# W1 kept raw and split per batch in the expert half of a graph-attention and mixture-of-experts kernel; b2 in three parts; the last GELUs ahead of a norm

## What is computed

```
Wh = layernorm(x) @ W.T
e  = leaky_relu(Wh@a1 [:,None] + Wh@a2 [None,:], 0.2), masked by adj > 0
x1 = x + elu(softmax(e) @ Wh)
xn = layernorm(x1)
two experts per batch: top 2 of softmax(rescaled softmax(mean(xn) @ Wr + br))
h  = gelu(xn @ W1[expert] + b1[expert]);  y = h @ W2[expert] + b2[expert]
out = x1 + layernorm(sum of gate * y + xn) * gamma + beta
```

## Time and profile before

| | us |
|---|---|
| median of 3 runs | 295.44 (293.95 to 296.98) |
| the profiled execution's own time | 294.31 |
| its span, first to last instruction | 292.5 |
| TensorE busy in it | 253.4 |
| VectorE busy in it | 234.6 |
| ScalarE busy in it | 222.7 |
| GpSimd busy in it | 154.2 |
| mean granted TensorE clock | 0.975 |

### The profile page before, as it was taken

How to read it: one execution, slowest core, us unless ns; L and a number is a source line. 1 busy time by engine, 2 the same in 40 slices (tenths; PEclk the granted TensorE clock), 3 DMA queues, 4 the chain that set the end, 5 groups by cost and what they waited for, 6 DMA issues and landing times.

```text
span 292.5 us, 6644 instructions
## 1 busy us (share of the span) xinstructions
PE 253.4 (87%) x1844; PEld 227.5 (78%) x1845; DVE 234.6 (80%) x668; ACT 222.7 (76%) x509; POOL 154.2 (53%) x239
## 2 busy tenths in 40 slices
PE   5639998999788989999987599499999999999962
PEld 3639987888778878899976347489999999999952
DVE  4297999999999999999997564607778767788756
ACT  2257898998988899999997449277878878888370
POOL 5242187788988897787548712112234432223544
PEclk9977999999999999999999979989999999999999
DMA  6999366543366236440000014832454445545222
GB/s 101 216 197 200 72 111 108 106 89 73 63 108 106 52 63 109 72 75 1 2 1 2 0 39 133 301 106 84 171 180 162 161 146 177 180 163 171 64 72 74
DMA packets 40670, 31.51 MB, mean 108 GB/s; under 512 B 2400, under 2 KB 36608, under 8 KB 40640
## 3 DMA queue, kind: packets, MB, share of 16 engines
q1 hardware_dynamic: 31936, 21.72, 23.3%
q0 software_dynamic: 8704, 9.45, 20.6%
HBM read 27.48 MB, written 4.20 MB: 108 GB/s over the span
## 4 chain that ended last, share of the span: by engine, by line
PE 38%; ACT 5%; issue 4%; POOL 3%; DVE 3%; SPq 3%; DMA 2%; POOLq 0%; DVEq 0%; ACTq 0%
PE banks L1359 16%; PE banks L1344 4%; PE banks L1346 4%; PE banks L1345 4%; PE banks L1222 4%; DMA w_pair<-w_parts 2%; ACT leaky L966 2%; PE banks L1175 1%; PE banks L1207 1%; POOL rstd L429 1%; PE banks L1199 1%; ACT leaky L1113 1%; ACT h_att L976 1%; SPq L321 1%; SPq L330 1%
## 5 line engine op out<-in xcount | busy, mean ns | idle before, releaser
L1222 PE MATMUL banks<-whx,prob_t 128*128 128x129 f32 x512 | 68.2, 277 | 3.7 <-ACT h_att L976 2.5
L1222 PEld LDWEIGHTS banks<-whx,prob_t 128*128 128x128 f32 x512 | 62.0, 192 | 6.8 <-issue 5.7
L416 POOL TENSOR_SCALAR x_all<-x_all,rstd,nb 128x128 f32<-128x128 f32 x60 | 44.2, 748 | 3.1 <-POOL nb L405 3.1
L1207 PE MATMUL banks<-ident,logit 128*128 128x128 f32 x256 | 37.6, 281 | 4.9 <-DVE logit L570 4.1
L481 POOL TENSOR_SCALAR veps<-mv 128x4 f32<-128x4 f32 x15 | 5.9, 393 | 64.0 <-DVE mv L834 64.0
L1001 ACT ACTIVATE prob_t<-banks 128x512 f32<-128x512 f32 x64 | 38.3, 638 | 0.9 <-PE banks L1207 0.8
L1103 ACT ACTIVATE logit<-logit,nb,rstd 128x128 f32<-128x128 f32 x60 | 24.8, 484 | 17.3 <-POOL nb L486 17.3
L1207 PEld LDWEIGHTS banks<-ident,logit 128*128 128x128 f32 x256 | 30.3, 145 | 6.2 <-DVE logit L570 6.0
L399 POOL TENSOR_TENSOR rstd<-var,minus_half 128x8 f32<-128x8 f32 (+1 forms) x20 | 33.7, 1684 | 0.4
L1344 PE MATMUL banks<-x2t_hi,w_pair 128*128 128x512 f32 x64 | 27.3, 426 | 4.1 <-DMA w_pair<-w_parts 3.9
L1359 PEld LDWEIGHTS banks<-w2s,masked_even 128*128 128x128 f32 x256 | 29.7, 192 | 0.5
(11 more groups left out here) (149 smaller groups left out, 560.8 us busy)
## 6 DMA issues: line engine op xcount, KB each, us to landing
adj_sb<-in_adj_dram POOLq DMA_DIRECT2D x16, 512.0 KB, 6.9
w_pair<-w_parts SPq DMA_DIRECT2D x30, 256.0 KB, 2.3
x_all<-in_x_dram SPq DMA_DIRECT2D x16, 256.0 KB, 2.8
w2r<-in_L_ffn_W_dram SPq DMA_DIRECT2D x32, 128.0 KB, 2.1
out_dram<-prob_t SPq DMA_DIRECT2D x15, 256.0 KB, 2.3
w_parts<-in_L_ffn_W_dram SPq DMA_DIRECT2D x1, 1024.0 KB, 9.2
b_mix<-b_spread POOLq DMA_DIRECT2D x1, 768.0 KB, 7.5
b_mix<-b_spread POOLq DMA_DIRECT2D x1, 256.0 KB, 4.2
```

Of the source, the lines that this page charges most:

```text
L416: nc.gpsimd.tensor_scalar(x_all[:, b, tile], x1_all[:, b, tile], rstd12[c % 4][:, 1, t:t + 1], nb2[c % 2][:, t:t + 1], ALU.mult, ALU.add). ...
L1207: last = nc.tensor.transpose(lt_ps[t % 2][:, c * P:(c + 1) * P], logit[:, t, c * P:(c + 1) * P], ident[:])
L1222: last = nc.tensor.matmul(into[:, 0:D + 1], prob_t[:, t, c * P:(c + 1) * P], whx[b % 3][:, c, 2:WHX], start=(c == 0), stop=(c == T - 1))
```

## The change

1. `w1_parts` becomes `w1_all`, the raw W1. The four splits on ScalarE and the four on GpSimd in the attention half are gone.
2. SyncE's load_w1 fetches the two chosen experts' raw W1 from DRAM into `w1_raw[batch % 2]`, 128 KB each. Two waits ahead of its first load are gone, and the load of batch b now waits for the low split of batch b-2.
3. ScalarE makes the high parts of a pair (`split_w1_hi`, 128x2x256) in step n for batch n+2, behind the GELUs of batch n+1. VectorE makes the low parts (`split_w1_lo`) in step n for batch n+2, behind aggregate3(n) and ahead of add_b2(n+2).
4. hidden_part(b) waits for the low split of batch b instead of for a DMA. Batch 0 has its own function (`first_hidden_part`): both products with the high part of W1 first, the four products with the low part at the end. Its raw weights are copied by GpSimd, its high parts made by ScalarE, straight from w1_all.
5. b2 goes out in three parts: batches 0 and 1, 2 to 4, and 5 to 15, the third one behind norm3(0).
6. The four GELUs of batch 15 stand ahead of norm_z(13).

```diff
             def load_w1(b):
                 par = b % 2
                 if b >= 2:
-                    sp.wait_ge(s_hid_ps, KC * (b - 1))
+                    sp.wait_ge(s_w1lo, b - 1)
                 for k in range(TOP_K):
                     e = sp.value_load(top_idx[b:b + 1, k:k + 1], min_val=0, max_val=E - 1)
-                    sp.dma_start(w1_pair[par][:, k].bitcast(F32), w1_parts[:, e].bitcast(F32)).then_inc(s_w1[par], 16)
+                    sp.dma_start(w1_raw[par][:, k, :], w1[e]).then_inc(s_w1[par], 16)
...
-            sp.wait_ge(s_w1lo, 4)
-            sp.wait_ge(s_x2t_ps, B)
             sp.wait_ge(s_idx, 1)
...
             for n in range(B + 1):
                 step(n)
-                if 5 <= n < 9:
-                    split_w1_lo(n - 5)
...
+            for k in range(TOP_K):
+                e = pool.value_load(top_idx[0:1, k:k + 1], min_val=0, max_val=E - 1)
+                nc.gpsimd.tensor_copy(w1_raw[0][:, k, :], w1_all[:, e]).then_inc(s_pick, 1)
...
             def step2(half, n):
                 if in_range(half, n):
                     norm3(half, n)
+                if isinstance(half, int) and n == 0:
+                    load_b2(2)
...
+            def split_w1_lo(half, n):
+                b, h, par = batch_at(half, n)
+                if isinstance(half, int) and b == 0:
+                    dve.wait_ge(s_pick, TOP_K)
+                if past(half, b, 2):
+                    dve.wait_ge(s_hid_ps, KC * (b - 1))
+                dve.wait_ge(s_w1hi, b + TOP_K)
+                nc.vector.tensor_tensor(w1_pair[par][:, :, 1, :], w1_raw[par][:], w1_pair[par][:, :, 0, :].bitcast(F32),
+                                        ALU.subtract).then_inc(s_w1lo, 1)
...
             router_steps["gated"] = rc[0]
+            split_w1_lo(0, 0)
...
             split_x2t_lo(0, 2)
+            split_w1_lo(0, 1)
...
                     split_x2t_lo(half, n + 3)
                 if in_range(half, n):
                     aggregate3(half, n)
+                if in_range(half, n + 2):
+                    split_w1_lo(half, n + 2)
                 if in_range(half, n + 2):
                     add_b2(half, n + 2)
...
-                if 4 <= n < 8:
-                    split_w1_hi(n - 4)
...
+            for k in range(TOP_K):
+                e = act.value_load(top_idx[0:1, k:k + 1], min_val=0, max_val=E - 1)
+                nc.scalar.copy(w1_pair[0][:, k, 0, :], w1_all[:, e]).then_inc(s_w1hi, 1)
...
+            def split_w1_hi(half, n):
+
+                b, h, par = batch_at(half, n)
+                act.wait_ge(s_w1[par], 32 * h + 32 * par)
+                if not isinstance(half, int) or b >= 2:
+                    act.wait_ge(s_hid_ps, KC * (b - 1))
+                nc.scalar.copy(w1_pair[par][:, :, 0, :], w1_raw[par][:]).then_inc(s_w1hi, 1)
...
             def step2(half, n):
                 if in_range(half, n + 1):
                     apply_gelu(half, n + 1)
+                if in_range(half, n + 2):
+                    split_w1_hi(half, n + 2)
                 if in_range(half, n + 3):
                     split_hi(half, n + 3)
...
             scale_w2(0, B - 1)
+            apply_gelu(0, B - 1)
             norm_z(0, END - 1)
-            apply_gelu(0, B - 1)
             norm_z(0, END)
...
-            def hidden_part(half, n, between=(None,) * KC):
+            def hidden_part(half, n):
                 b, h, par = batch_at(half, n)
-                first = isinstance(half, int) and b == 0
-                if not first:
-                    pe.wait_ge(s_w1[par], 32 * h + 32 * par)
                 pe.wait_ge(s_x2lo, b + 1)
+                pe.wait_ge(s_w1lo, b + 1)
```

More of the change, by code:

```diff
@@ L129, in gat_moe_kernel @@
         b2_spread = nc.dram_tensor("b2_spread", [B, D], F32, kind="Internal")
-        w1_parts = sb("w1_parts", [P, E, 2, F], F32R)
+        w1_all = sb("w1_all", [P, E, F])
+        w1_raw = [sb(f"w1_raw{i}", [P, TOP_K, F]) for i in range(2)]
         w2r = [sb(f"w2r{i}", [P, TOP_K, FC, D]) for i in range(2)]
@@ L215, in gat_moe_kernel @@
         s_b2_out = sem("b2_rows_spread")
-        s_b2mix = [sem("b2_mix_loaded0"), sem("b2_mix_loaded1")]
+        s_b2mix = [sem(f"b2_mix_loaded{i}") for i in range(3)]
         s_n2e = sem("norm2_end_chain")
-        s_pick = [sem("first_w1_copied0"), sem("first_w1_copied1")]
+        s_pick = sem("first_w1_copied")
         s_x1b = sem("x1b_ready")
@@ L417, in scale_x2 @@
                                             nb2[c % 2][:, t:t + 1], ALU.mult, ALU.add).then_inc(s_x2, 1)
[L419 to L423, removed]
             def norm2_last_tile(t):
@@ L465, in _, with load_b2 @@
             pool.wait_ge(s_b2_out, 16)
-            for i, part in enumerate((slice(0, B2_FIRST), slice(B2_FIRST, B))):
+            def load_b2(i):
+                part = slice(B2_PARTS[i], B2_PARTS[i + 1])
                 nc.gpsimd.dma_start(b2_mix[:, part, :], b2_spread[part, :].rearrange("(a b) d -> a b d", a=1).to_broadcast(
                     [P, part.stop - part.start, D])).then_inc(s_b2mix[i], 16)
+            load_b2(0)
+            load_b2(1)
             def norm3(half, n):
@@ L796, in add_b2 @@
                 b, h, par = batch_at(half, n)
-                if isinstance(half, int) and b == B2_FIRST:
-                    dve.wait_ge(s_b2mix[1], 16)
+                if isinstance(half, int) and b in B2_PARTS[1:3]:
+                    dve.wait_ge(s_b2mix[B2_PARTS.index(b)], 16)
                 nc.vector.tensor_tensor(x_all[:, b, :].rearrange("p (t d) -> p t d", t=T),
@@ L1326, in mix_b2 @@
                 nc.tensor.matmul(r2_ps[0:B, 128:128 + D], w_dense_t[:], b2_sb[:], start=True, stop=True).then_inc(s_rps, 1)
-            def hidden_part(half, n, between=(None,) * KC):
+            def first_hidden_part(between):
+                pe.wait_ge(s_x2lo, 1)
+                for kc in range(KC):
+                    k, columns = kc // FC, slice(kc % FC * P, (kc % FC + 1) * P)
[3 more added lines that the diff above has]
+                    nc.tensor.matmul(hid_ps[kc], hi, x2t_lo[0][:], start=False, stop=False)
+                    if between[kc] is not None:
+                        between[kc]()
+                pe.wait_ge(s_w1lo, 1)
+                for kc in range(KC):
+                    k, columns = kc // FC, slice(kc % FC * P, (kc % FC + 1) * P)
+                    nc.tensor.matmul(hid_ps[kc], w1_pair[0][:, k, 1, columns], x2t_hi[0][:], start=False,
+                                     stop=True).then_inc(s_hid_ps, 1)
+            def hidden_part(half, n):
                 b, h, par = batch_at(half, n)
-                first = isinstance(half, int) and b == 0
-                if not first:
-                    pe.wait_ge(s_w1[par], 32 * h + 32 * par)
                 pe.wait_ge(s_x2lo, b + 1)
+                pe.wait_ge(s_w1lo, b + 1)
                 for kc in range(KC):
                     k, c = kc // FC, kc % FC
-                    if first and c == 0:
-                        pe.wait_ge(s_pick[k], 1)
-                    if not isinstance(half, int) or b >= 1:
-                        pe.wait_ge(s_hid, KC * (b - 1) + kc + 1)
+                    pe.wait_ge(s_hid, KC * (b - 1) + kc + 1)
                     columns = slice(c * P, (c + 1) * P)
@@ L1347, in hidden_part @@
                                      stop=True).then_inc(s_hid_ps, 1)
-                    if between[kc] is not None:
-                        between[kc]()
             def out_part(half, n):
```

19 lines of the change are left out of this document (6 added, 13 removed).

## The result

The changed kernel takes 368.19 us (median of 4 runs, 367.87 to 369.5), the kernel before 295.73 us (median of 4, one more than in the table above, 293.95 to 296.98): ratio 1.246, 95% interval 1.239 to 1.254. Forecast were 359 us with a range of 342 to 374; the time is inside the range and 9 us over the forecast, nearest to rival 1 (367 us). The profiled execution took 369.5 us and has a span of 367.7.

What follows compares the result with a forecast made beforehand. The prediction took the expert half to be bound by TensorE alone. From 294.3 us: -3.9 (attention half), +4.7 (entry), +50.4 (waits), +13.8 (clock), 0 (end) gave 359.3, say 359 us; range 342 to 374.

Steps and rivals of the forecast that it cites:

- rival 1: Expert half: the clock falls in every gap, 1.8 us each, 367 us in all; chance 0.20.
- the closed chain: Expert half, each batch: output(n), sum_z(n), four more VectorE groups, W1 low part, hidden(n+2); 4.2 us.
- 4.2 us per batch, 12 new waits, none for hidden(15): Expert half: TensorE waits for W1's low part, 12 x 4.2 = 50.4 us new; hidden(15)'s wait near 0.
- The clock, 1.2 us a gap: Expert half: slow clock after 13 gaps, 15.6 us less 1.8 paid today, +13.8 us (bounds -1.8 to +21.6).
- The upper value of 1.8: Expert half: most slow-clock time per gap, in us, from nine matmuls 0.43 us apart instead of 0.23 to 0.24.
- ScalarE's copy and the raw loads at nothing: Expert half: ScalarE's high part per batch and SyncE's W1 loads from DRAM are ready early; cost 0.
- The attention half, -3.9 us: Attention half: without ScalarE's four copies and GpSimd's four subtracts, -3.9 us (bounds -2.0 to -3.9).
- rival 4: Attention half gives nothing, as another engine holds its beat at the same length: 363 us; chance 0.04.
- the lower bound of -2.0: Attention half: the gain in us if only ScalarE's copies count.
- The entry, +4.7 us: Start of expert half: hidden(1) waits 2.8 us for W1's low part, GELUs 2 us late; bounds +2.5 to +6.5.
- The end, 0: Kernel's end: last GELUs could start some 3 us earlier, but VectorE's tail needs norm_z(14); 0 (bounds -3 to +0.6).
- Rival 3, faster: Expert half: W1's low part ready before output(n) ends, beat stays 6.33 us, 289 us; chance 0.03.

Runs made afterwards that it cites:

- experiment 1: Changed kernel with VectorE's low split of W1 for batch n+2 moved ahead of sum_z(n): 291.73 us, ratio 0.989 to the kernel before.
- experiment 3: Changed kernel with the low split of W1 directly behind sum_z(n), ahead of add_beta: 324.68 us, ratio 1.101 to the kernel before.
- experiment 2: Changed kernel with 14 idle matmuls on TensorE ahead of each hidden product from batch 1 on, results unused: 345.3 us, ratio 1.171.
- experiment 4: On experiment 1, four 128x512 copies on ScalarE put back into the attention half, output unread: 292.29 us.
- experiment 5: On experiment 1, four 128x512 subtracts on GpSimd put back into the attention half, output unread: 294.74 us, ratio 0.996.
- experiment 6: On experiment 1, both ScalarE's four copies and GpSimd's four subtracts put back into the attention half, outputs unread: 295.43 us, ratio 0.997.
- experiment 8: On experiment 1, W1's splits for batch 1 and the low split for batch 2 moved earlier in the entry: 286.92 us, ratio 0.970.
- experiment 7: On experiment 1, the last four GELUs put back behind norm_z(13), as in the kernel before: 293.0 us, ratio 0.991.
- experiment 9: On experiment 8, b2's rows sent out in two parts (batches 0 to 3 and 4 to 15), both at once: 285.87 us, ratio 0.965.
- experiment 10: On experiment 8, eight idle matmuls in TensorE's pauses inside hidden(0), results unused: 287.59 us, ratio 0.972.

## Why the prediction was right, and where its size was off

**What bounds the half; the closed chain.** Right. TensorE bound it before (busy 87.35 of 87.40 us); experiment 1 shows that the order alone breaks it, and experiment 3 that the loss follows the length of the chain: four groups fewer, 4.2 becomes about 2.0 us.

**4.2 us per batch, 12 new waits, none for hidden(15).** Right: gaps of 3.81 to 4.14 us, the beat without a slow clock 10.53 us as forecast, 4.3 in experiment 2, and hidden(15) without idleness.

**The clock, 1.2 us a gap.** This term is the one that was mis-sized. Twelve beats at full clock would be 12 x 10.53 = 126.4 us; they took 148.78, so 22.4 us are the clock's, and 1.3 more in hidden(14), which took 4.17 us instead of 2.84: 23.7 us for 13 gaps, 1.8 each, where I had put 15.6. Experiment 2 gives 22.9 in another way; its beats with the clock held up are 10.60 us, 0.8 us more in twelve, and with that it is 23.7 too. The weighing down to 1.2 went wrong in both of its reasons. The first was that the clock fell only when the work had already come back, so that the gap was at the edge. It fell in twelve of the thirteen; four of them show the same late fall and the other eight were slow from the first matmul. The second was the stretch 280 to 284 us, which kept its clock. The waits in it are a third as long:

```profile
281.32 0.49 PE L1364 MATMUL banks<-x_all,ident 128*128 128x128 f32 x2 [1.37 <-ACT leaky L1113]
283.13 3.81 PE L1379 MATMUL banks<-w2s,leaky 128*128 128x128 f32 x32 [1.33 <-ACT leaky L1113]
```

The upper value of 1.8 was not well read either. The prediction took it from matmuls at 190.02 and 190.45, which the rows above don't show:

```profile
190.02 0.63 PE L1344 MATMUL banks<-x2t_hi,w_pair 128*128 128x512 f32 x1
190.45 0.63 PE L1345 MATMUL banks<-x2t_lo,w_pair 128*128 128x512 f32 x1
...
193.32 3.73 PE L1359 MATMUL banks<-w2s,leaky 128*128 128x128 f32 x32
```

From 188.87 to 193.32 this hidden product took 4.45 us, 1.6 more than 2.84, not 1.8. And it was no upper bound: in four beats of 13.3 to 13.5 us the low clock reached into the output product, and they are up to 2.95 us longer than 10.53. Rival 1 had the mechanism better than the forecast, the clock falling nearly every time. That its 1.8 a gap is also the mean found here is in part luck, as the single gaps cost between 0 and 2.95 us.

The page "TensorE: Matmul & The Clock Gate" of the Trainium skill, section "HAM oscillation — how this bites in real kernels", has the clock fall in each of a series of waits of 3 to 5 us. Twelve of the thirteen gaps here agree, one (10.53 us) does not, and the sum by that rule (367 us, rival 1) was nearer than the one by my weighing of two rows.

**ScalarE's copy and the raw loads at nothing.** Right: the high part is ready 5.4 us ahead in the beat shown, and no wait on a DMA stands ahead of a hidden product.

**The attention half, -3.9 us.** The sum is right (-3.8), and the exponentials of h now stand 8.75 us apart (59.44 to 111.95 in six steps), so rival 4 falls. The split is not right: not 2.0 us of ScalarE's copies and 1.9 of shift_neg's wait, but nearly all of it the wait: the subtracts alone cost 3.0 us, the copies beside them nothing more (experiments 4, 5 and 6), and the longer subtract makes up the 0.9 that are left. So the lower bound of -2.0, "if only the copies count", was on the wrong part. The page "SBUF — State Buffer" of the Trainium skill, section "Who interferes with whom", which the prediction named, lets a VectorE instruction with two inputs in SBUF and a GpSimd instruction that reads SBUF hold each other up, by which came first. Experiment 5 agrees: the subtract came first (71.33 against 71.52), and shift_neg ended when it ended.

**The entry, +4.7 us.** Measured +5.6 to hidden(1), and hidden(1) itself ran with a slow clock behind its own wait of 3.83 us, 1.4 us more: 7.0 together, above the bound of 6.5. The step that failed is leaving the clock out of the middle value though a gap of the known size was forecast there. Of the +5.6 some 4.95 lie between hidden(0) and hidden(1), near the 4.7. The other 0.7 lies in the router ahead of hidden(0), which the prediction had put at nothing: from the exponential of batch 14 to hidden(0) are 17.9 us instead of 17.3. The same stretch is 16.4 us in experiment 1 and 16.3 in experiment 8, so it differs from kernel to kernel; why stays open.

**The end, 0.** Without hidden(14)'s clock it is -0.6. The GELUs did move, and in experiment 7, where the last output product moves by 3.0 us, the end moves by 0.8 only; that VectorE's tail takes the rest is argued, not shown.

By the terms: 359.3 + 8.1 (clock) + 0.2 (the slow clock paid before is 1.6 us, not 1.8) + 2.3 (entry) - 0.6 (end) + 0.1 (attention) = 369.4 us; the profiled time is 369.5.

**Rival 3, faster.** It decided by whether the subtract stands before or behind sum_z, and said 289 us; experiment 1, which does just that, takes 291.73. Most of the rest lies in the entry: there hidden(1) comes 5.3 us later than before and its slow clock costs 1.3 more, 6.7 us against a term of 4.7.

## What to carry to other kernels

Where the engine that bounds the time waits for another one's product, look at what stands ahead of the producing instruction in its queue: an instruction that itself waits for the bound engine's last output closes a ring, and its length is paid in every step, however little work it is. Move the producer ahead of that wait before anything is made shorter. And price a repeated gap on TensorE at the gap plus the slow clock behind it: here 4.2 + 1.8 us, nearly half more.

## What the runs showed of the hardware that I had not expected

- Gaps of only 1.6 to 1.9 us in every beat of about 8.3 us brought the clock down too, in five of twelve beats (experiment 3), at some 1.65 us each. Two waits of 1.37 and 1.33 us near the end of the kernel before did not. Why in these beats and not in the others stays open.
- The same instructions on TensorE met a clock of 0.50 in one kernel's entry and of 1.00 in another's (experiments 8 and 9). The one with 1.00 was faster by about 1 us in the median.
- Idle matmuls in a wait made a kernel 6% faster (experiment 2); in the entry they brought nothing that the medians show (experiment 10).
- A tiny VectorE instruction paid for the rest of a GpSimd subtract: 0.14 us became 0.89 beside one of 1.05 us, and 1.12 beside one of 1.28 us.
- ScalarE's four copies of 0.62 us in a chain that binds the attention half cost 0.2 us together, and nothing beside GpSimd's subtracts, where it waits 1.35 us for shift_neg without them and 0.82 with them (experiments 5 and 6).
